# Splitting the last output projections by head, adding the second batch's expert sums on TensorE, and reading these sums back in four pieces

## The reference, cut to what matters

```python
xn  = layernorm(x)
A   = attention_16_heads(xn)          # W_Q, W_K, W_V, W_O with biases, causal
# the second branch, on the same xn:
r   = xn + rotary_attention(rmsnorm(xn)) @ wo      # 16 heads, 4 key/value heads
h   = rmsnorm(r)
moe = sum over the 4 chosen of 32 experts e:  w_e * (silu(h@weg_e) * (h@weu_e)) @ wed_e
out = x + A + r + moe + shared_expert(h)
```

## Time and profile before

| | us |
|---|---|
| median of 3 runs | 802.19 |
| lowest and highest | 800.16, 802.36 |
| the profiled execution's own time | 799.75 |
| its span, first to last instruction | 797.9 |

### The profile page before, as it was taken

One profiled execution on the slowest core, in us unless ns is written; L12 is line 12 of the kernel. 1 busy time (PEld: TensorE's weight loads), 2 busy tenths in 40 slices (PEclk: granted clock), 3 DMA queues, 4 the chain that ended last, 5 costly groups with the idle time before them and its releaser, 6 DMA issues.

```text
span 797.9 us, 14383 instructions
## 1 busy us (share of the span) xinstructions
PE 739.1 (93%) x4615; PEld 661.8 (83%) x4615; DVE 555.4 (70%) x1699; ACT 485.5 (61%) x1218; POOL 486.4 (61%) x564
## 2 busy tenths in 40 slices
PE   1899999999999999999889895999999999999995
PEld 1678888888888888889778794999989999999984
DVE  5878888797888877666888663555556565556575
ACT  3776778677777875676344452565566655665551
POOL 3679777776877784335234876365655856656553
PEclk9999999999999999999999998999999999999998
DMA  5000000000100199201000622377777776677543
GB/s 168 27 14 28 14 15 26 22 15 21 41 28 29 26 320 267 83 2 53 13 14 21 189 82 86 92 172 182 176 185 169 197 176 146 154 167 179 95 88 104
DMA packets 103491, 77.51 MB, mean 97 GB/s; under 512 B 6950, under 2 KB 102266, under 8 KB 103418
## 3 DMA queue, kind: packets, MB, share of 16 engines
q1 hardware_dynamic: 92234, 63.19, 28.1%
q0 software_dynamic: 10752, 12.74, 9.5%
q10 hardware_dynamic: 432, 0.67, 0.3%
HBM read 51.75 MB, written 24.82 MB: 96 GB/s over the span
## 4 chain that ended last, share of the span: by engine, by line
PE 62%; DVE 13%; ACT 9%; POOL 6%; issue 4%; DMA 4%; SPq 1%; DVEq 0%; POOLq 0%; ACTq 0%
PE j L823 17%; PE ob L823 8%; PE zb L823 8%; PE s L823 8%; PE t L956 6%; ACT probs L1104 4%; PE j L910 3%; DVE probsT L1373 2%; POOL probs L676 2%; PE zb L910 2%; PE j L918 2%; ACT rope_swapped L1136 2%; ACT rope_swapped L1137 2%; POOL x_slots_dram L687 2%; PE ob L910 2%
## 5 line engine op out<-in xcount | busy, mean ns | idle before, releaser
L676 POOL TENSOR_SCALAR probs<-probs,inv_sum 128x128 f32<-128x128 f32 (+3 forms) x256 | 148.9, 594 | 170.8 <-DVE inv_sum L1364 166.5
L1104 ACT ACTIVATE probs<-probs,neg_max 128x128 f32<-128x128 f32 (+3 forms) x256 | 143.1, 559 | 131.5 <-DVE neg_max L1358 130.1
L823 PE MATMUL s<-k_heads,q_heads 128*128 128x256 f32 (+2 forms) x576 | 139.0, 362 | 3.3 <-DVE neg_max L1358 2.8
L1358 DVE CUSTOM_DVE_ANT_0 probs<-s,mask 128x128 f32<-128x128 f32 (+3 forms) x256 | 120.0, 485 | 11.6 <-PE s L823 6.5
L712 POOL DMA_INDIRECT moe_sum_dram<-late,slot_tokens x64 | 101.4, 1585 | 39.1 <-ACT late L1181 28.4
L1373 DVE TENSOR_TENSOR probsT<-t,probsT 128x384 fp32r<-128x384 f32 (+2 forms) x192 | 101.4, 548 | 12.1 <-ACT probsT L1111 11.1
L956 PE MATMUL t<-ident,probs 128*128 128x128 f32 x640 | 95.0, 275 | 13.7 <-POOL probs L676 12.3
L1111 ACT ACTIVATE probsT<-t 128x384 fp32r<-128x384 f32 (+2 forms) x192 | 89.9, 486 | 26.1 <-PE t L956 25.9
L823 PEld LDWEIGHTS s<-k_heads,q_heads 128*128 128x128 f32 x576 | 91.7, 191 | 9.8 <-DVE neg_max L1358 6.1
L956 PEld LDWEIGHTS t<-ident,probs 128*128 128x128 f32 x640 | 74.9, 141 | 23.1 <-POOL probs L676 15.2
L823 PE MATMUL zb<-probsT,v_heads 128*128 128x512 f32 (+2 forms) x351 | 68.1, 338 | 1.4 <-DVE probsT L1373 0.9
(11 more groups left out here) (255 smaller groups left out, 1576.9 us busy)
## 6 DMA issues: line engine op xcount, KB each, us to landing
x_slots_dram<-mask SPq DMA_DIRECT2D x1, 8480.0 KB, 41.4
late<-x_slots_dram SPq DMA_DIRECT2D x32, 265.0 KB, 4.7
late<-in_L_ffn_weg_dram SPq DMA_DIRECT2D x64, 128.0 KB
late<-in_L_ffn_weu_dram SPq DMA_DIRECT2D x64, 128.0 KB
late<-in_L_ffn_wed_dram SPq DMA_DIRECT2D x64, 128.0 KB
moe_sum_dram<-mask SPq DMA_DIRECT2D x2, 1152.0 KB, 9.0
raw_qk<-in_L_ffn_wq_dram SPq DMA_DIRECT2D x16, 128.0 KB, 2.2
raw_o<-in_L_ffn_wo_dram SPq DMA_DIRECT2D x8, 256.0 KB, 2.7
```

The source lines that it names most:

```text
L676: pool.tensor_scalar(piece, piece, rinv[:, u % 2, i:i + 1], 1.0, ALU.mult, ALU.mult).then_inc(p_norm, 1)
L823: m = pe.matmul(dst, lhs(a), rhs(b), start=first and i == 0, stop=last_ and i == 2, skip_group_check=skip)
L1104: act.activation(piece, piece, ACT.Exp, bias=nmax[:, u % 2, i:i + 1], scale=-1.0, accum_out=rsum[:, u % 2, i:i + 1]).then_inc(e_done, 1)
L1358: ve.tensor_tensor_reduce(pr[:, u % 2, P_OFF[i]:P_OFF[i] + width], bS[i % 2][:, 0:width], mask_t[:, S - width:S], INV_SCALE, BIG, ALU.add, ...
```

## The change

The projections `O(64)` and `O(65)` are split by head: the six matmuls of head 62 go ahead of the last attention product, the six of head 63 stay behind it. `O(63)` moves from step 63 to step 62, between `attend(62)` and the last transposes; DVE's add of it moves to the end of step 62. DVE's four adds of the expert sums of batch 1 go; PE adds these sums into the banks of `O(64)` and `O(65)` with eight matmuls whose stationary operand is the identity (plain float32, 256 columns each). The expert sums are read back in four DMAs of 512 KB, batch 1 first, with a semaphore for each batch. The order of the four banks follows.

```diff
+    def outs_of(n):
+        return [n] if 2 <= n < UNITS - 1 else [UNITS, UNITS + 1] if n == UNITS - 1 else []
@@ ring_of
-        out = [("O", n)] if n >= 2 else []
         if n >= UNITS:
-            return out
+            return []
+        out = [("O", m) for m in outs_of(n)]
...
-        return g[1] + over_from(n) + g[2] + out + g[3] + g[4] + own + [("Z", n)] + g[5] + g[6]
+        return g[1] + over_from(n) + g[2] + out + g[3] + g[4] + own + [("Z", n)] + (
+            [("O", n + 1)] if n == UNITS - 2 else []) + g[5] + g[6]
@@ SP
-            for j in range(2):
-                sp.wait_ge(y_out[j], 16 * (PAIRS - SHARED))
-                sp.dma_start(macc[j], moe_sum[j][P:P + B * S, :].rearrange("(t p) d -> p t d", p=P)).then_inc(acc_in, 16)
+            for b in reversed(range(B)):
+                for j in range(2):
+                    sp.wait_ge(y_out[j], 16 * (PAIRS - SHARED))
+                    sp.dma_start(macc[j][:, b * TB:(b + 1) * TB, :],
+                                 moe_sum[j][P + b * S:P + (b + 1) * S, :].rearrange("(t p) d -> p t d", p=P)
+                                 ).then_inc(acc_in[b], 16)
@@ POOL
-            pool.wait_ge(acc_in, 32)
+            pool.wait_ge(acc_in[0], 32)
@@ PE
+            def add_experts(n):
+                o = n - 2
+                half, b = o % 2, o % GS // 4
+                pe.wait_ge(acc_in[b], 32)
+                for t in range(2):
+                    for j in range(2):
+                        pe.matmul(bR[BANK["O", n]][:, t * D:(t + 1) * D], ident[:, :], macc[j][:, b * TB + 2 * half + t, :],
+                                  start=False, stop=False, skip_group_check=True)
-            def out_project(n, t, it):
+            def out_project(n, t, it, heads=(0, 1)):
...
-                    kept(pe, ("Z", 2 * m_ + 1), it)
+                    kept(pe, ("Z", 2 * m_ + heads[-1]), it)
...
-                for j in range(2):
+                for j in heads:
...
@@ PE, step
                     guests(n, 2)
+                    if n == UNITS - 1:
+                        last_unit()
+                        return
...
                     attend(n, it)
+                    if n == UNITS - 2:
+                        out_project(n + 1, 0, it)
+                        out_project(n + 1, 1, it)
                     guests(n, 5)
...
+            def last_unit():
+                for t in range(2):
+                    out_project(UNITS, t, None, (0,))
+                turn_probs(UNITS - 1, 2, None)
+                for t in range(2):
+                    out_project(UNITS + 1, t, None, (0,))
+                attend(UNITS - 1, None)
+                for n in (UNITS, UNITS + 1):
+                    add_experts(n)
+                for n in (UNITS, UNITS + 1):
+                    for t in range(2):
+                        out_project(n, t, None, (1,))
             windows(pe, step)
-            for n in (UNITS, UNITS + 1):
-                out_project(n, 0, None)
-                out_project(n, 1, None)
@@ DVE, add_out
-                if n >= UNITS:
-                    ve.wait_ge(acc_done, NT // 2)
@@ DVE, step
-                    add_out(n, it)
+                    if n < UNITS - 1:
+                        add_out(n, it)
...
                         probs_lo(n + 1, 1, it)
+                    if n == UNITS - 2:
+                        add_out(n + 1, it)
                     route_3(n)
@@ DVE, route_1
-                if n == UNITS - 1:
-                    ve.wait_ge(acc_in, 32)
-                    kept(ve, ("O", n))
-                    for j in range(2):
-                        if j:
-                            ve.wait_ge(acc_done, NT // 4)
-                        for t in range(TB, NT, 2):
-                            ve.tensor_tensor(accB[:, t:t + 2, :], accB[:, t:t + 2, :], macc[j][:, t:t + 2, :],
-                                             ALU.add).then_inc(acc_done, 1)
```

More of the change, by code:

```diff
@@ L396, in attention_pair_moe_kernel @@
         rt_exp, idx_done, rows_done, et_done = sem("router_exp"), sem("dest_ready"), sem("rows_ready"), sem("blocks_ready")
-        z_in, sc_out, acc_in = sem("scratch_zeroed"), sem("rows_scattered"), sem("moe_sum_in")
+        z_in, sc_out, acc_in = sem("scratch_zeroed"), sem("rows_scattered"), [sem("moe_sum_in0"), sem("moe_sum_in1")]
         sh_in, xs_in = sem("w_shared_in"), [sem("x_slots_in0"), sem("x_slots_in1")]
@@ L403, in attention_pair_moe_kernel @@
         waits_passed = sem("waits_passed")
-        acc_done, acc_done0, out_sem = sem("moe_added"), sem("moe_added_first"), sem("out_written")
+        acc_done0, out_sem = sem("moe_added_first"), sem("out_written")
         def until(eng, s, count, it=None, per=0):
@@ L980, in out_project @@
                 if half == 0 and t == 0:
-                    kept(pe, ("Z", 2 * m_ + 1), it)
+                    kept(pe, ("Z", 2 * m_ + heads[-1]), it)
                     until(pe, w_done, JOB[(f"O{hp}", a)] + 1, it, JOBS_W)
-                if t == 0:
+                if t == 0 and heads[0] == 0:
                     vacant(pe, ("O", n), it)
                 tok = (2 * half + t) * P
-                for j in range(2):
+                for j in heads:
                     m = mm3(bR[BANK["O", n]][:, t * D:(t + 1) * D],
@@ L989, in out_project @@
                             lambda p: w_o[:, hp, p, j, :], t == 0 and j == 0, t == 1 and j == 1, skip=True)
-                if t == 1:
+                if t == 1 and heads[-1] == 1:
                     m.then_inc(o_mm, 1)
```

## The result

| | before | after |
|---|---|---|
| median of 18 runs, us | 802.12 | 797.57 |
| lowest and highest | 799.16, 804.86 | 793.92, 801.01 |
| profiled execution: own time, span | 799.75, 797.9 | 794.28, 792.5 |

The ratio is 0.9942 with a 95% interval of 0.9925 to 0.996, so the kernel is 4.7 us faster (3.2 to 6.0). The forecast was a gain of 4.8 us and a time of 797.4.

The account below looks back on a forecast made before the run. The end was taken to be bound by DVE's four adds ahead of z_part, then 24 matmuls at half clock. Last add 4.9 us earlier less 0.1 for output gives 802.19 - 4.8 = 797.4 us, 8-in-10 range 794.9 to 800.3.

Parts of the forecast that it names:

- Order of the end: At the end, DVE's z_part(63) stood behind four adds until 788.14, though ACT's high part was ready at 785.43.
- Part 1: O(63) into step 62: twelve matmuls (1.44 us) leave step 63, transposes start 0.32 late, attend(63) loses 0.2.
- Part 2: Head 62's twelve matmuls ahead of attend(63) fit in PE's waits and cost nothing; otherwise 1.44 us.
- Part 3: DVE's adds (5.7 us) leave the path, PE's eight identity matmuls take 3.5; last add starts 4.9 earlier.
- The clock: PE pauses at most some 0.6 us from 779, keeping full clock: 24 matmuls take 2.88 us there, 5.50 before.
- POOL: With DVE's adds gone, POOL's four adds at the end take 5.1 us instead of 6.8; z_part isn't held.
- Part 4: Read-back in four: last scatter ends 1.8 us earlier; closer issue of the two last output DMAs costs 0.1.
- (b): Rival: read-back pieces land one after another, POOL ends last and holds the outputs; gain 3.3 us, 798.9; chance 0.17.
- (c): Rival: PE's clock drops after all, identity matmuls take 7.0 us; gain 0.3, 801.9; chance 0.10.
- (d): Rival: late read-back makes PE idle before add_experts and the clock halves; 3.3 us later, 805.5; chance 0.04.
- (e): Rival: DVE's z_part stays late for another reason, say POOL's adds; 800.0; chance counted with (b).
- The sum: Last add 4.9 us earlier, less 0.1 at the output DMAs: 4.8 gained, 802.19 to 797.4.

Follow-up runs that it names:

- e5: Kernel before with only DVE's four adds of the expert sums moved behind z_part(63): 797.66 us against 803.22, ratio 0.9946.
- e2: Changed kernel with DVE's four adds back ahead of z_part(63), two reads of 1 MB, no identity matmuls: 799.93 us against 803.22, ratio 0.9973.
- e3: Kernel before plus identity matmuls in place of DVE's adds and the read-back in four, without head split or O(63) move: 800.83 us against 802.47, ratio 0.9967.
- e4: Kernel before plus nine unused float32 matmuls in PE's wait between attend(63) and O(64): 802.0 us against 803.22, ratio 0.9983.
- e6: Changed kernel with batch 1's expert sums added by DVE behind z_part(63) instead of by PE: 798.23 us against 802.47 before, ratio 0.9953.
- e9: Changed kernel with the read-back in two DMAs of 1 MB and one semaphore: 796.52 us against 803.94 before, ratio 0.9932.
- e10: Changed kernel with POOL first summing batch 1's two tensors, four identity matmuls, and DVE's O(63) add behind the last probs_lo: 794.9 us against 803.94 before.

## Why the prediction was right

By its own steps, all from attend(62)'s start:

- **Order of the end.** Right: z's low part was held by DVE's adds alone. e5 shows it with one edit (z 12.22 to 9.58).
- **Part 1.** The first transposes went from 2.91 to 3.34 (0.43, forecast 0.32), turn_probs(63, 2) from 5.28 to 5.31 (forecast unmoved), attend(63) from 6.72 to 6.83 (0.11, forecast 0.2). The 1.79 of attend(62) in this part is too short as well, for the reason given under part 3.
- **Part 2.** Right: PE still waited 0.22 and 0.37 us for DVE beside the split matmuls, so they cost nothing. e2 against before and e3 against the change put the value of split and move together at 2.44 and 1.24.
- **Part 3.** Identity matmuls 3.46, forecast 3.5, by the rows of L918. The step that was off: attend(63) took 1.85 + 0.22 = 2.07 and not 1.79. I took the 1.57 of an attend that PE reached without a pause; after a wait for DVE its nine matmuls take 1.85, as the row of attend(62) said. Part of that is how the chain counts: without a pause it starts a group where the one before ends, which overlaps it (attend(61) is 1.57 in the chain and 1.74 in the timeline), and behind a pause there is nothing to overlap with. The twelve matmuls of e4 show it too: 1.69 behind the wait, 1.45 for the next. That is 0.28 late. And the last add didn't follow PE, which was done at 788.9, but DVE's own add ahead of it (788.37 + 0.70, then 0.12). Together with the 0.1 that part 1 gave back, the last add came at 14.10 instead of 13.88.
- **The clock.** 1.00 to 790, as forecast. e4 gives its price alone, 2.36; I had 2.6 (5.50 - 2.88).
- **POOL.** Four adds in 5.09, forecast 5.1. The rule of the Trainium skill on the port pair (SBUF — State Buffer, "SBUF: two separate sides") holds in e6 as well: one add of DVE beside POOL at 1.67, those after POOL's end at 0.68. The exclusion isn't quite of whole instructions, though: one after the other, the eight adds of before would be 7.88 by my estimate (4 x 0.69 + 4 x 1.28), and they took 6.84 (782.50 to 789.34). In e6 DVE's first add ended 0.55 after POOL's last (790.05 and 789.50), 0.13 less than an add alone; eight times 0.13 is about the difference.
- **Part 4.** Too hopeful and without effect: from the first read to the second it was 4.79 (769.82 to 774.61) against 5.87, so 1.1 earlier and not 1.8. POOL's adds of batch 0 began at 6.40 instead of 6.62. e9 shows that even two reads would have done. The case of the Trainium skill for large DMAs (DMA: Bandwidth & Descriptors, "Rules for kernel authors"), my rival (b), didn't come up either: the pieces overlapped, the last issued at 775.6 and landed 5.8 later, and the two reads of 1 MB in e9 were no faster (6.44 against 6.34).
- **Rivals.** (b): POOL was done at 786.6, 1.8 before DVE's add of O(64). (c) didn't happen here; by its own sum (794.35 against 794.44) it would have gained 0.1 and not 0.3. (d): PE had no wait for the read-back. (e): no; z_part was not held by POOL.
- **The sum.** 4.64 less 0.07 at the output is 4.57 in the traces, 4.55 between the medians and 4.7 by the ratio; forecast 4.8.

So the mechanism was right, and the sizes that were off add up to 0.2 us of M: the last add was to start 4.86 earlier (794.66 - 789.8), and it was 4.64.

What the forecast didn't see is how little of the gain hangs on PE doing the adds. With DVE's adds only moved behind z, M is 15.58 without split and move (e5, whose read-back landed 0.5 late) and 14.98 with them (e6). With the sums on PE it is 15.34 (e3) and 14.10. PE in DVE's place is worth 0.24 or 0.88, and the timed runs resolve neither. The identity matmuls themselves lay on the path for 1.6 us, though POOL had idled 3.5 us ahead of its adds.

## What to carry to other kernels

When an engine waits for one short step, look first at what is queued ahead of that step on its engine, and move it before moving work to another engine. Where PE waits as long as it did here (4.2 us), look at the granted clock behind the wait: filling the wait with matmuls made the stretch from z to the last add 2.4 us shorter. The chain of waits names one path; before removing what it names, work out when the next one arrives (e10: 0.17 us earlier, so 0.15 gained of 0.6).

## What was not expected of the hardware

Executions of one kernel differ by 5.7 to 7.1 us (18 runs each). In the changed kernel the difference arises ahead of the end: its two profiles start attend(62) at 775.09 and 780.23, and M is 14.10 and 14.11. 2.5 of these are there by the router's logits (first matmul on gate_cols at 368.6 and 371.1). Another part follows a pause of PE that was the same in both: 2.33 and 2.31 us of waiting for POOL. In the first the clock stayed at 1.00, in the second it fell to half within 2 us of PE's new start (windows of the first, then of the second; columns as in the earlier trace rows):

```profile
448.00:450.00 2.00, 2.00 (x16) 1.92 (x16) 0.94 (x3) 1.04 (x2) 1.70 (x2) 1.00 0.81 289
450.00:452.00 2.00, 2.00 (x15) 1.84 (x15) 0.96 (x5) 1.35 (x5) 1.39 (x3) 1.00 0.19 68
```

```profile
450.00:452.00 2.00, 1.67 (x14) 1.67 (x15) 1.43 (x4) 1.51 (x3) 1.53 (x3) 0.93 0.90 295
452.00:454.00 2.00, 2.00 (x6) 1.57 (x6) 1.73 (x7) 0.64 (x4) 1.70 (x2) 0.50 0.39 142
454.00:456.00 2.00, 2.00 (x13) 1.85 (x12) 0.66 (x2) 1.00 (x3) 1.39 (x3) 0.72 0.27 100
```

So a pause of 2.3 us may or may not cost the clock, while the 4.2 us of the earlier trace rows and e2 did, and the 1.56 us of e5 did not. In the kernel before, 2.08 us of waiting up to 394.46 were followed by a granted clock of 0.50 in 396 to 398. What decides it, and where the first 2.5 us arise, I haven't settled. These differences are why a change of 1 us at the end is seen in the trace and hardly in the times.
